# Fourth attention: one map of two heads per score unit, keys on their own 32 rows, output work behind both units

## What is computed

```python
q = (x @ Wq).reshape(b, s, H, 2 * D)       # H = 16 heads, D = 16
k = (x @ Wk).reshape(b, s, KVH, 2 * D)     # KVH = 4 key heads
v = (x @ Wv).reshape(b, s, KVH, D)
q = _rope(q); k = _rope(k)
energy = jnp.einsum('bqhad,bkhad->bahqk', qd, kd)       # a: two maps per head
energy = jnp.where(causal, NEG, energy)
scores = jax.nn.softmax(energy / np.sqrt(D), axis=-1)
diff = scores[:, 0] - lam * scores[:, 1]
diff = jax.nn.softmax(jnp.where(causal, NEG, diff), axis=-1)
att = jnp.einsum('bhqv,bvhd->bqhd', diff, v)
att = att * rsqrt(mean(att * att) + EPS) * rms_w * (1 - LAM_INIT)
return att.reshape(b, s, E) @ Wo
```

## Time and profile before

| | us |
|---|---|
| median of 3 runs | 3296.48 |
| lowest, highest | 3294.09, 3298.33 |
| span of the profiled execution | 3294.2 |
| of it, the stage of the changed loop (2226 to 2760) | 534 |

### The profile page before, as it was taken

The page is one execution under the profiler, slowest core; times in us unless marked ns, Lnnn a source line. Parts: engine busy times, 40 slices in busy tenths (PEclk is TensorE's granted clock), DMA queues, the critical chain, the costliest instruction groups (busy, mean ns, idle before and its releaser), DMA issues. The chain is left out here.

```text
span 3294.2 us, 44074 instructions
## 1 busy us (share of the span) xinstructions
PE 2885.3 (88%) x14664; PEld 2204.1 (67%) x14672; DVE 1903.6 (58%) x4499; ACT 1284.9 (39%) x3325; POOL 127.8 (4%) x96
## 2 busy tenths in 40 slices
PE   7999699989999999999598877798778886799997
PEld 6888544446777767777476665547666665678776
DVE  3555533334454554545645857647777775677777
ACT  2222155544344443443222132208666774223232
POOL 0000000000000000000022000001111110000000
PEclk8999799999999999999799988899888887799998
DMA  3000200000000000000200000100000001000000
GB/s 146 6 6 3 103 1 0 0 0 7 3 0 3 3 3 3 0 3 0 86 0 0 0 1 0 40 1 32 16 13 16 16 10 78 38 1 0 0 0 25
DMA packets 25115, 54.76 MB, mean 17 GB/s; under 512 B 3552, under 2 KB 21728, under 8 KB 23392
## 3 DMA queue, kind: packets, MB, share of 16 engines
q1 hardware_dynamic: 25056, 54.02, 4.4%
HBM read 39.33 MB, written 2.10 MB: 13 GB/s over the span
## 5 line engine op out<-in xcount | busy, mean ns | idle before, releaser
L1592 PE MATMUL psum<-l3a_kr,l3a_qr 128*128 128x128 f32 (+1 forms) x1024 | 271.3, 395 | 7.0 <-ACT l3a_pr L1697 3.7
L1697 ACT ACTIVATE l3a_pr<-psum,l3a_nm 128x128 f32<-128x128 f32 (+1 forms) x512 | 207.2, 431 | 167.0 <-DVE l3a_nm L1796 166.8
L108 DVE TENSOR_TENSOR x_sb<-psum,x_sb 128x512 f32 (+2 forms) x48 | 41.7, 869 | 317.6 <-PE psum L845 135.5
L1592 PEld LDWEIGHTS psum<-l3a_kr,l3a_qr 128*128 128x128 f32 x1024 | 179.6, 218 | 42.0 <-issue 17.0
L1796 DVE TENSOR_REDUCE l3a_nm<-psum 128x2 f32<-128x256 f32 (+1 forms) x256 | 130.1, 550 | 92.0 <-PE psum L1594 90.8
L363 ACT ACTIVATE l0a_pr<-psum,l0a_nm 128x128 f32<-128x128 f32 (+1 forms) x256 | 86.6, 421 | 235.9 <-DVE l0a_nm L417 235.9
L656 DVE TENSOR_TENSOR l0f_hg<-l0f_sq,psum 128x512 f32<-128x512 f32 x128 | 87.7, 687 | 156.0 <-ACT l0f_sq L598 152.2
L2009 PE MATMUL psum<-l3f_x_hi,l3f_w_hi 128*128 x384 | 154.5, 402 | 7.2 <-DVE l3f_w_lo L2092 7.2
L890 ACT ACTIVATE l1a_pr<-psum,l1a_nb,l1a_rq 128x128 f32<-128x128 f32 (+1 forms) x256 | 127.2, 509 | 85.0 <-DVE l1a_nb L943 85.0
L2010 PE MATMUL psum<-xT,l3f_w_hi 128*128 x384 | 152.8, 398 | 0.0
L2011 PE MATMUL psum<-l3f_x_hi,l3f_w_lo 128*128 x384 | 152.1, 396 | 0.0
(11 more groups left out here) (420 smaller groups left out, 7172.2 us busy)
## 6 DMA issues: line engine op xcount, KB each, us to landing
w_l3f_all<-l3f_all_dram SPq DMA_DIRECT2D x1, 9216.0 KB, 25.8
l3a_qr<-l3a_q_all SPq DMA_DIRECT2D x32, 256.0 KB, 2.5
w_l0f_w<-l0f_w_dram SPq DMA_DIRECT2D x2, 2048.0 KB, 9.8
w_l1f_all<-l1f_all_dram SPq DMA_DIRECT2D x1, 2560.0 KB, 8.8
x_sb<-x_dram SPq DMA_DIRECT2D x1, 2048.0 KB, 8.4
l0a_xc<-xT SPq DMA_DIRECT2D x8, 256.0 KB, 2.5
w_l1a_q<-l1a_q_dram SPq DMA_DIRECT2D x1, 2048.0 KB, 8.1
w_l1a_k<-l1a_k_dram SPq DMA_DIRECT2D x1, 2048.0 KB, 12.6
```

The source lines that it names most:

```text
L1592: mm(S[n % 2][:, a, t * P:t * P + (t + 1) * P], qr[:, a, r, t * P:(t + 1) * P], kr[:, g, a, 0:(t + 1) * P], start=True, stop=False)
L1697: last = nc.scalar.activation(pr[:, m % 2, a, j, s], S[j][:, a, s], ACT.Exp, bias=nm[:, j, t, a:a + 1], accum_out=sums[:, m % 2, a, j, t:t ...
```

## The change

A score unit becomes one map `a` of both heads of a pair: unit n = 2m + a. Each score matmul takes the 32 partitions of its head (`tile_position=(row, 0)`), so the two heads of a pair stand on different rows of the array and write different banks, `S[a][:, 0]` and `S[a][:, 1]`. The four mask matmuls stand together behind the four score matmuls. `kr` is one plain copy of the batch's keys (`stage_keys`), with no zeros. On TensorE `scores(2m+1)` stands directly behind `scores(2m)`, ahead of the output work of steps 6 and 7; on ScalarE `output` stands behind both exponentials; on VectorE `maxima(15)` and the key copy come ahead of `output`.

```diff
@@ -1486,7 +1486,7 @@
         sem = lambda name: ctx.enter_context(nc.semaphore("l3a_" + name))
         q_all = sb("q_all", [P, A, R, TOK])
         qr = sb("qr", [P, A, R, T])
-        kr = sb("kr", [P, G, A, T])
+        kr = sb("kr", [P, A, T])
         va = sb("va", [P, NT, G, V1])
         lam = sb("lam", [P, 2, H])
         lprod = sb("lprod", [P, 2, H, HD])
@@ -1522,7 +1522,7 @@
         proj_out = sem("proj_out")
         k_rotated = sem("k_rotated")
         q_staged = [sem("q_staged%d" % r) for r in range(R)]
-        k_spread = sem("k_spread")
+        k_staged = sem("k_staged")
         lam_ready = sem("lam_ready")
         s_ps = sem("s_ps")
         nm_ready = sem("nm_ready")
@@ -1581,17 +1581,22 @@
                         last.then_inc(proj_ps, 1)
 
                 def scores(b, n):
-                    r, g = n // G, n % G
-                    if g == 0:
+
+                    m, a = n // 2, n % 2
+                    r = m // 2
+                    if n % G == 0:
                         pe.wait_ge(q_staged[r], b * 16 + 16)
-                    if n < 4:
-                        pe.wait_ge(k_spread, b * 4 + g + 1)
+                    if n == 0:
+                        pe.wait_ge(k_staged, b + 1)
                     pe.wait_ge(p_exp, b * H + n + 1)
-                    for a in range(A):
-                        for t in range(TT):
-                            mm(S[n % 2][:, a, t * P:t * P + (t + 1) * P], qr[:, a, r, t * P:(t + 1) * P],
-                               kr[:, g, a, 0:(t + 1) * P], start=True, stop=False)
-                            last = mm(S[n % 2][:, a, 2 * t * P:(2 * t + 1) * P], c["idb"], c["maskb"], start=False, stop=True)
+                    for t in range(TT):
+                        for j in range(2):
+                            row = 32 * (2 * (m % 2) + j)
+                            mm(S[a][:, j, t * P:t * P + (t + 1) * P], qr[row:row + 32, a, r, t * P:(t + 1) * P],
+                               kr[row:row + 32, a, 0:(t + 1) * P], start=(t == 0), stop=False, tile_position=(row, 0))
+                    for t in range(TT):
+                        for j in range(2):
+                            last = mm(S[a][:, j, 2 * t * P:(2 * t + 1) * P], c["idb"], c["maskb"], start=False, stop=(t == TT - 1))
                     last.then_inc(s_ps, 1)
 
 
@@ -1640,6 +1645,7 @@
 
                     for m in range(NG):
                         scores(b, 2 * m)
+                        scores(b, 2 * m + 1)
                         before = (None, None)
                         if m == 6 and not first:
                             pe.wait_ge(pt_ready, b * H + 2 * (m - 3) + 1)
@@ -1649,7 +1655,6 @@
                             pe.wait_ge(pt_ready, b * H + 2 * (m - 3) + 2)
                             project_output(b - 1)
                             before = (None, z_ready)
-                        scores(b, 2 * m + 1)
                         if not first or m >= 3:
                             turn(b, m - 3, before)
                         if not first or m >= 4:
@@ -1687,14 +1692,14 @@
                 act.sem_inc(pt_ready, 2)
 
                 def exponentials(b, n, opening):
-                    m, j = n // 2, n % 2
+                    m, a = n // 2, n % 2
                     act.wait_ge(nm_ready, b * H + n + 1)
                     if not (opening and m < 2):
                         act.wait_ge(dif_ready, b * NG + m - 1)
-                    for a in range(A):
+                    for j in range(2):
                         for t in range(TT):
                             s = slice(t * P, t * P + (t + 1) * P)
-                            last = nc.scalar.activation(pr[:, m % 2, a, j, s], S[j][:, a, s], ACT.Exp, bias=nm[:, j, t, a:a + 1],
+                            last = nc.scalar.activation(pr[:, m % 2, a, j, s], S[a][:, j, s], ACT.Exp, bias=nm[:, a, t, j:j + 1],
                                                         accum_out=sums[:, m % 2, a, j, t:t + 1])
                     last.then_inc(p_exp, 1)
 
@@ -1723,9 +1728,9 @@
                 def sequence(b, opening):
                     for m in range(NG):
                         exponentials(b, 2 * m, opening)
+                        exponentials(b, 2 * m + 1, opening)
                         if m == 6 and not opening:
                             output(b - 1)
-                        exponentials(b, 2 * m + 1, opening)
                         if not opening or m >= 2:
                             second(b, m - 2, opening)
                         if not opening or m >= 3:
@@ -1757,8 +1762,7 @@
                 dve.wait_ge(set_up, 3)
                 nc.vector.tensor_scalar(nlam[:, :], nlam[:, :], -LAM_INIT, None, ALU.add).then_inc(set_up, 1)
                 nc.vector.tensor_scalar(gain[:, :], w["rms"], 1.0 - LAM_INIT, None, ALU.mult).then_inc(set_up, 1)
-                nc.vector.memset(va[:, :, :, HD:V1], 1.0)
-                nc.vector.memset(kr[:, :, :, :], 0.0).then_inc(set_up, 1)
+                nc.vector.memset(va[:, :, :, HD:V1], 1.0).then_inc(set_up, 1)
                 dve.wait_ge(set_up, 6)
                 dve.sem_inc(on_raw, 1)
 
@@ -1784,10 +1788,8 @@
                     dve.wait_ge(proj_out, j * NP + NP)
                     nc.vector.tensor_tensor(k_all[:, :, chunk], k1[:, :, 0, :], k1[:, :, 1, :], ALU.add).then_inc(k_rotated, 1)
 
-                def spread_keys(b):
-                    for g in range(G):
-                        rows = slice(32 * g, 32 * g + 32)
-                        nc.vector.tensor_copy(kr[rows, g, :, :], k_all[rows, :, bass.ds(b * T, T)]).then_inc(k_spread, 1)
+                def stage_keys(b):
+                    nc.vector.tensor_copy(kr[:, :, :], k_all[:, :, bass.ds(b * T, T)]).then_inc(k_staged, 1)
 
                 def maxima(b, n):
                     dve.wait_ge(s_ps, b * H + n + 1)
@@ -1813,12 +1815,12 @@
                         h = 4 * (n % G) + n // G
                         last = nc.vector.scalar_tensor_tensor(ratio[:, i, j, :], sums[:, i, 0, j, :], nlam[:, h:h + 1], rec[:, i4, 1, j, :], ALU.mult, ALU.mult)
                     ratios = st.inc(last)
-                    if with_output:
-                        output(b - 1)
                     if between is not None:
                         maxima(b, between + 1)
                     if with_keys:
-                        spread_keys(b + 1)
+                        stage_keys(b + 1)
+                    if with_output:
+                        output(b - 1)
                     st.wait(ratios)
                     for j in range(2):
                         for t in range(TT):
@@ -1888,7 +1890,7 @@
                 for j in range(NCH):
                     rotate(j)
                 dve.wait_ge(k_rotated, NCH)
-                spread_keys(0)
+                stage_keys(0)
                 st.begin(0)
                 sequence(0, True, False)
                 st.pad()
```

## The result

The changed kernel takes 3323.9 us (median of four runs, 3319.86 to 3324.99) against 3295.28 before (four runs). The ratio is 1.0084, with a 95% interval of 1.0070 to 1.0099: slower by 28.6 us, where 3251 was forecast, with a range up to 3302.

The account below looks back on a forecast made before the run. No engine was full; waits between engines bounded the kernel. Steps gave -7.1 a batch, the clock +1.0, leaving -6.1: -43 over seven batches, -2 in the opening, 3294.2 to 3249, 3251 as median; 8-in-10 range 3212 to 3302.

Parts of the forecast that it names:

- TensorE stays at half clock: Rival, whole stage: each pair costs TensorE 8.2, a batch 73, 5 more than now; 3330 to 3346; chance 0.13.
- 0.4 of such a pair a batch (+1.0): Clock price in the sum: a pair at half clock costs 8.2, 2.5 above ScalarE's 5.65; 0.4 a batch, +1.0.
- The overlap of two row tiles: Score unit on TensorE: two heads side by side, 1.1 at full clock against 1.76 without overlap, 2.2 at half clock.
- The key copy: VectorE, step 7: one instruction of 0.44 in place of four, 1.76; -1.3 inside that step.
- Step 7: Pair step with TensorE late, at half clock: 10.5 against 11.85 (-1.35).
- step 0: Step behind `Wo`: VectorE's add and 2.81, then ScalarE's second softmax and one copy; 5.6 to 6.0 against 8.03 (-2.0).
- VectorE's wait in step 6: Sign: VectorE's idle time of 5.32 ahead of the maxima in step 6 should fall below 1.
- Step 6: Step with output transposes, still waiting for ScalarE's output copy: stays at 13.5 (-0.2); growth would make the forecast wrong.
- Step 1: Step with VectorE's `measure`: 6.8 against 8.85 (-2.05), as writing scores at half clock in front of it goes.
- Steps 2 to 5: Plain steps and VectorE's norm steps: 12.01 becomes 11.4 (-0.6), 13.70 becomes 12.8 (-0.9).
- The rival with the clock up: Step 7 takes 7.0, no pair falls to half clock: -11.6 a batch, 3213; chance 0.17.
- The drain: TensorE's price for changing between row-tiled and full matmuls: four changes a pair make 0 to 0.65, hidden under ScalarE.

## Why the prediction was wrong, point by point

**The likeliest case was the wrong one; a rival came true.** I gave 0.13 to "TensorE stays at half clock" and put it at 3330 to 3346; measured 3323.9. Its working held: a pair was to cost 8.2 and cost 7.89, a batch 73 and was 71.67. Its reason did not: it put the loss in the plain steps, "where TensorE will be idle more often", and in two of them TensorE was busy for 15.80 of 15.80 us at 0.50. That this case stood among the rivals with about the right price is partly luck.

**The step that failed** is the sentence in which I counted "0.4 of such a pair a batch (+1.0)" at half clock. I had judged the clock by idle time alone and taken for granted that a tiled matmul keeps TensorE as awake as a full one. About seven pairs of a batch ran at half clock and not 0.4, and with that the sentence by which TensorE's own work falls from 5.6 to 4.2, "under ScalarE's 5.65", held for about one pair a batch; the others cost 7.89. What had held the clock was the score work on 128 rows: with it put back, the stage is at 0.86 and the kernel 58 us faster.

**The row that should have made me ask** is the last of the earlier trace rows: 4 us of a fully busy TensorE at 0.50. It says nothing of tiles, since that work stood on 128 rows, but it shows that being busy isn't enough. I used it for the rival and not for the sum. A prediction about TensorE's load has to ask at which clock it will be carried, before it asks how long the work is.

**What held, in part by luck.** The overlap of two row tiles: 1.18 a unit, 1.1 forecast; 2.12 at half clock, 2.2 forecast. The forecast came from eight weight loads one after another, and there it was right by luck: the eight loads are over in 0.52 (0.93 at half clock), while the eight passes take 0.85 (1.58) up to the masks. The loads are not the pace; what is was not parted. The key copy 0.42 (0.44). Step 7 10.58 (10.5), at half clock as forecast, and step 0 6.03 (5.6 to 6.0), at full clock. VectorE's wait in step 6 gone, as said.

**Sizes that were off.** Step 6 was to stay at 13.5 and took 14.83, by which the forecast had itself said it would be wrong: at half clock TensorE's scores are late for VectorE's step 5 too, whose two maxima wait 0.83 and 0.84 for them. Step 1 was to be 6.8 and took 7.95, all of it TensorE. Steps 2 to 5 were to take 24.2 and took 32.28. The -0.2 of step 6 overlooked that ScalarE's copy needn't have moved at all; left in place it was worth 14 us to the order.

**The order** was right in kind and too large in size. Alone it gave 10 us where 7.1 a batch were forecast for the whole. The regrouped unit with its masks together, which gave about 19, was not in the sum at all: I had priced four masks at 0.055 wherever they stand. The rival with the clock up has a slip besides: 6.1 and 3.5 and 1.0 are 10.6 a batch and not 11.6, so it should have stood at about 3220 and not 3213.

**The drain** was bounded at 0 to 0.16 a change. The run with 64 rows shows 2.86 from first score matmul to masks, and 0.54 from the masks to the next unit, where four masks of 128 rows among themselves are 0.11 apart each at half clock; 0.1 remains for a change, inside the bounds. (The Trainium skill, TensorEngine Tiling (Array Packing), Key Properties, says that a change of mode drains TensorE; the run with one small matmul a unit agrees: its units start 2.04 apart instead of 1.61, 0.43 for one small matmul in two passes and two changes.)

```profile
2442.88 0.38 PE L1593 MATMUL psum<-l3a_kr,l3a_qr 32*128 32x1 f32 x2
2443.19 1.58 PE L1597 MATMUL psum<-l3a_kr,l3a_qr 128*128 128x128 f32 x8
...
2444.92 0.38 PE L1593 MATMUL psum<-l3a_kr,l3a_qr 32*128 32x1 f32 x2
```

## What to carry to other kernels

Before packing small matmuls onto row tiles, look at the granted clock of the stretch and at who is the bound there. If another engine sets the pace, zero-padded matmuls over all 128 rows can be the cheaper ones, because TensorE may stay at 2.4 GHz with them and fall to 1.2 GHz without: here the tiles saved 0.43 a unit at full clock (1.61 to 1.18), the stage's clock went from 0.86 to 0.53, and the kernel was 58 us slower. Undo a change part by part even if it loses as a whole: of its four parts the order of the units and steps without the output copy gained 25 us (3295.64 - 3270.62) and the regrouped unit about 19, while moving the copy lost 14 and the tiles 58. The two gains, with one more move on VectorE, take 1.65% off the kernel before.

## What the runs showed of the hardware

- Score matmuls on 32 or 64 rows, with four changes of tiling mode a pair, left the stage at 0.53 to 0.58 of the full clock; on 128 rows, mostly zeros, with as many changes, it was 0.88. In the run with 32 rows and sixteen changes TensorE was at half clock while busy for 100 us out of 100.
- Sixteen changes of tiling mode a pair, with small tiled matmuls in between, brought the clock to 0.54 even with all full-row work kept; four a pair left it at 0.88.
- Two float32 row tiles run side by side, and so do their weight loads: the eight passes of a unit took 0.85 at full clock and 1.58 at half, their eight loads 0.52 and 0.93.
- Four bf16 masks behind four float32 matmuls make a unit 0.15 shorter than one mask behind each.
